# The routing section of a two-layer mixture-of-experts kernel: another way to the gather indices, and another order of loads

## The chip, the cores and the metric

One Trainium2 chip, one of its cores. The metric is the device time of one execution in microseconds, the median of several runs. The profile is that of one execution.

## The reference

There are 1024 tokens of 128 features, in 8 batches of 128. Two layers run one after the other, all in float32; the change lies in the first.

```python
# layer 0: a projection with a weight for each batch, then experts with top 2 of 8
out  = einsum('btc,oc->bto', x, W_base) + b_base
lora = einsum('bter,eor,be->bto', einsum('btc,erc->bter', x, As), Bs, w)
c    = out + 2 * lora
top_w, top_idx = top_k(softmax(c @ router_w.T), 2); top_w /= sum(top_w) + 1e-9
y    = relu(c @ w1[e].T + b1[e]) @ w2[e].T + b2[e]        # hidden width 512
x    = x + sum over the two chosen e of top_w * y
# layer 1: each batch by the expert of its argmax (silu(up) * gate, width 256), then
# every one of 8 experts takes its best 256 tokens (gelu, width 512), scattered back by add
```

## The kernel before

**Routing.** The logits of the router don't need the projected tokens: router and projection are folded into one 128x8 matrix for each batch (`gmat`), and eight matmuls on `xT_sb` give all logits (L468). VectorE picks the top two (L897 to L906). TensorE counts, with triangular and all-ones matrices, how many tokens stand in front of each in its expert (L498 to L503). This gives each (token, choice) a slot in one list of 2048, sorted by expert. VectorE splits the slot's number into block (`blk`, 16 of them) and place in the block (`loc`), and makes two one-hots: `slot1h` (128 places x 16 pairs of choice and batch, L926) and `blk1h` (16 x 16 blocks, L921). `blkv` holds `blk1h` times the token's number in its batch (part 0, on ScalarE, L744) and times the constant `dval`, which is 128 c + 1024 k (part 1, on VectorE, L923). Sixteen matmuls (L512) turn them into the two parts of each slot's number. VectorE adds the parts (L937), turns them to int32 as `sidx` (L938, where a result is scattered to) and masks them to `gidx` (L940, the token to be gathered). `slot1h` compares `loc` with `cols0`, an iota table of 128x2048 in bf16 that ScalarE writes (L736).

**Projection.** It runs beside this. ScalarE scales `b_sb` by the batch's weights (L734). TensorE puts W_base into two banks, by a matmul of `wb_sb` with the identity (L473), and adds the low-rank part (L477, `sum_weights`). ScalarE copies the sum to `w_eff` (L739); TensorE multiplies the tokens by it (L483, `project`); ScalarE copies the result to `c_tok` (L742). The SP queue stores `c_tok` to `rows0` in DRAM, in two halves (L335).

**Experts of layer 0.** Each of the 16 blocks of 128 slots is gathered by GpSimd with an indirect DMA from `rows0` (L394). It waits for `gidx` and for both stores (L383, L384). TensorE turns the block (L523) and runs 23 pairs of block and expert: `up` (L538) and `down0` (L548). In iteration j it turns block j, runs `up` of pair j - 1 and `down0` of pair j - 2; up to 24 full-width matmuls on ones (`keep_warm`, L516) stand before the first. VectorE copies each pair's w1 to a ring (`w1_now`, L951) and keeps the results (L976, L982); GpSimd scatters finished blocks.

**The SP queue**, in order: `first`, `xT`, `consts`, `second`, `crow`, all of w1 (2064 KB), 6 of 8 experts of w2 (1536 KB, L331); then the waits for both halves of `c_tok` and the two stores of 256 KB (L335), the other two experts of w2 (512 KB, L337), `b2`, `gate_w`, `c1`. From L349 on it waits for `cexp` of VectorE and then, paced by the turned blocks, loads the weights of layer 1. TensorE waits for all of w2 before its first `down0` (L562).

**After it**: layer 1 (L566 to L700), which nothing in the diff touches.

Of the kernel before, what the change touches and what calls it, by code (L numbers as in the profile page):

```python
# [27 lines left out]
E = 8  # L28
# [32 lines left out]
           ("slotj", NPAIR), ("dval", K * NC), ("cval", NC), ("same", P), ("coarse", 2), ("steps", STEPS)]  # L61
# [16 lines left out]
def constants():  # L78
# [21 lines left out]
    put("dval", (P * c + T * k).reshape(1, -1))  # L100
# [8 lines left out]
def adaln_moe(nc, xT, x, first, second, rows, w1, w2, cond_w, gate_w, v1, c1, v2, consts, out):  # L109
    with ExitStack() as ctx:  # L110
# [24 lines left out]
        b_sb = sb("b_sb", [P, C])  # L135
# [56 lines left out]
        blkv = sb("blkv", [P, K * NC, 2, NB], BF16)  # L192
        idxf = sb("idxf", [P, NB])
# [77 lines left out]

        dve = sem("dve_steps")
# [47 lines left out]
        def _(sp):  # L320
# [6 lines left out]
            load(b_sb[:], second, in_second)  # L327
            load(crow_sb[:], rows[:, CNR:CNR + NC * E], in_crow)
            load(w1_sb[:], w1, in_w1)
            W2H = 6 * NF * C  # L330
            load(w2_sb[:, 0:W2H], w2[:, 0:W2H], in_w2)  # L331
# [49 lines left out]
        def _(pool):  # L381

# [61 lines left out]
        def _(pe):  # L444
# [26 lines left out]
            pe.wait_ge(in_const, 16)  # L471
            for g in range(2):
                pe.matmul(bank[2 + g][:], wb_sb, ident.unsqueeze(1).to_broadcast([P, 4, P]), start=True, stop=False)  # L473

            def sum_weights(g):
                pe.wait_ge(bsc_ready, 4 * g + 4)
                pe.matmul(bank[2 + g][:], a_sb, bsc[:, 512 * g:512 * g + 512], start=False, stop=True).then_inc(w_summed, 1)  # L477

            def project(g):

                pe.wait_ge(w_eff_ready, g + 1)
                for c in range(4 * g, 4 * g + 4):
                    mm = pe.matmul(bank[5 + g][:, P * (c % 4):P * (c % 4) + P], xT_sb[:, P * c:P * c + P],  # L483
                                   w_eff[:, P * c:P * c + P], start=True, stop=True)
# [10 lines left out]
            sum_weights(1)  # L495
            pe.wait_ge(mask_ready, 1)
# [19 lines left out]
            keep_warm(bank[3], 24)  # L516
# [37 lines left out]
            for j in range(NPAIR + 2):  # L554
# [6 lines left out]
                if j == 2:  # L561
                    pe.wait_ge(in_w2, 32)  # L562
# [166 lines left out]
        def _(act):  # L729
# [3 lines left out]
            for c in range(NC):  # L733
                act.activation(bsc[:, C * c:C * c + C], b_sb[:], ACT.Identity, scale=cr2[:, c:c + 1]).then_inc(bsc_ready, 1)  # L734
            act.wait_ge(in_const, 16)
            act.activation(cols0, const("iota").unsqueeze(2).to_broadcast([P, P, K * NC]), ACT.Copy).then_inc(cols_ready, 1)  # L736
# [15 lines left out]
            act.activation(cols1, const("iota").unsqueeze(2).to_broadcast([P, P, K * NC]), ACT.Copy).then_inc(cols_ready, 1)  # L752
# [107 lines left out]
        def _(v):  # L860
# [61 lines left out]
            v.wait_ge(blk1h_ready, 1)  # L922
# [280 lines left out]
```

## Time and profile before

| | us |
|---|---|
| median of 3 runs | 170.29 |
| lowest and highest of them | 168.7, 170.41 |
| the profiled execution | 169.11 |
| its span in the trace | 167.3 |
| busy in it: TensorE, VectorE, ScalarE, GpSimd | 141.0, 92.5, 72.8, 64.4 |

The span runs from the first instruction to the last; 1.81 us of the execution's own time lie around it. Times of rows are microseconds from the span's start. PE is TensorE, PEld its weight loads, DVE VectorE, ACT ScalarE, POOL GpSimd; SPq is the queue that issues DMAs. "Issue" is time for which the profile shows nothing that was waited for.

### The profile page before, as it was taken

How to read it: one execution, taken by the hardware profiler on the slowest of the kernel's cores; microseconds unless marked ns; L12 is line 12 of the kernel's file. 1: busy time of each engine (PE TensorE's matmuls, PEld its weight loads, DVE VectorE, ACT ScalarE, POOL GpSimd, SP SyncE). 2: the span in 40 equal slices, each digit the busy share in tenths (PEclk: the TensorE clock that was granted, in tenths of full speed). 3: DMA queues.
4: the chain of work that ended last, by engine and by line, in shares of the span. 5: the costliest groups of instructions: out<-in, count | busy, mean ns of one | idle time of the engine just before them, and what ended most of it. 6: DMA issues, size and time to landing. Idle time of an engine off the chain costs nothing.

```text
span 167.3 us, 3393 instructions
## 1 busy us (share of the span) xinstructions
PE 141.0 (84%) x1044; PEld 117.8 (70%) x1044; DVE 92.5 (55%) x302; ACT 72.8 (44%) x223; POOL 64.4 (38%) x67
## 2 busy tenths in 40 slices
PE   7998959999999999994999720188889988899991
PEld 3756439999988999743999610045479877788990
DVE  0489391565553554415767988764353368436182
ACT  1678325777765656301478540000145444434100
POOL 0000376544476445624000000015777777776000
PEclk9999996999999999999699995559999999999999
DMA  5999827998898921127069240000122345515804
GB/s 163 355 427 345 254 67 218 325 297 277 281 299 246 313 108 47 35 64 220 0 264 402 92 133 0 0 2 21 50 50 66 93 135 173 174 52 157 233 17 125
DMA packets 20419, 27.52 MB, mean 164 GB/s; under 512 B 2034, under 2 KB 14706, under 8 KB 20146
## 3 DMA queue, kind: packets, MB, share of 16 engines
q1 hardware_dynamic: 17410, 22.78, 41.2%
q0 software_dynamic: 1920, 4.00, 8.0%
q10 hardware_dynamic: 1072, 0.52, 1.1%
q8 instruction: 9, 0.15, 0.4%
q14 instruction: 8, 0.07, 0.1%
HBM read 20.71 MB, written 6.59 MB: 163 GB/s over the span
## 4 chain that ended last, share of the span: by engine, by line
PE 55%; DMA 14%; DVE 12%; POOL 9%; issue 6%; ACT 1%; DVEq 0%; ACTq 0%; POOLq 0%
PE bank L538 10%; PE bank L548 9%; PE bank L679 6%; PE bank L580 5%; PE bank L689 4%; PE bank L669 4%; DMA xs<-rows,gidx 4%; DVE bsc L1060 4%; DMA xg<-rows,idx 4%; POOL xg L420 3%; DMA rows<-c_tok 2%; POOL plane L427 2%; PE bank L450 2%; DMA got<-picked 2%; PE bank L589 2%
## 5 line engine op out<-in xcount | busy, mean ns | idle before, releaser
L763 ACT ACTIVATE hT<-bank,w_now 128x128 f32<-128x128 f32 x92 | 26.2, 368 | 13.6 <-PE bank L538 13.6
L394 POOL DMA_INDIRECT xs<-rows,gidx x16 | 15.5, 969 | 27.7 <-DMA rows<-c_tok 18.8
L538 PE MATMUL bank<-xg,w_now 128*128 (+1 forms) x184 | 25.5, 283 | 0.0
L548 PE MATMUL bank<-w_sb,hT 128*128 (+1 forms) x184 | 25.1, 281 | 0.3 <-ACT hT L763 0.3
L548 PEld LDWEIGHTS bank<-w_sb,hT 128*128 128x128 f32 x184 | 23.2, 198 | 0.5 <-ACT hT L763 0.5
L538 PEld LDWEIGHTS bank<-xg,w_now 128*128 128x128 f32 x184 | 23.2, 198 | 0.5 <-issue 0.5
L450 PE MATMUL bank<-ones 128*128 128x512 bf16 x81 | 22.0, 418 | 1.1 <-DVE ones L877 1.1
L842 ACT ACTIVATE h1T<-bank,c_sb 128x256 f32<-128x256 f32 x32 | 13.4, 470 | 19.0 <-PE bank L669 19.0
L399 POOL DMA_INDIRECT picked<-y,sidx x16 | 15.4, 962 | 13.3 <-DVE y L982 12.1
L420 POOL DMA_INDIRECT xg<-rows,idx x16 | 16.9, 1058 | 6.3 <-issue 4.0
L669 PE MATMUL bank<-xgT,v_sb 128*128 128x256 f32 x64 | 16.5, 383 | 0.5 <-ACT xgT L833 0.5
L976 DVE TENSOR_TENSOR yt<-bank,b_sb 128x128 f32<-128x128 f32 x23 | 6.7, 291 | 18.0 <-PE bank L548 15.8
L679 PEld LDWEIGHTS bank<-v_sb,h1T 128*128 128x128 f32 x128 | 15.3, 192 | 1.0 <-ACT h1T L842 0.8
L679 PE MATMUL bank<-v_sb,h1T 128*128 128x128 f32 x128 | 15.9, 277 | 0.1
L427 POOL DMA_INDIRECT plane<-x_sb,idx x12 | 13.6, 1136 | 3.7 <-issue 2.7
L450 PEld LDWEIGHTS bank<-ones 128*128 128x128 bf16 x81 | 8.2, 109 | 9.4 <-issue 2.2
L431 POOL TENSOR_TENSOR hlfv<-hlf1h,cst 128x128 bf16<-128x128 bf16 x1 | 0.8, 776 | 34.5 <-DVE hlf1h L1099 34.5
L1123 DVE TENSOR_TENSOR yb<-bank,c2b_sb 128x128 f32<-128x128 f32 x16 | 4.7, 291 | 15.4 <-issue 9.3
L669 PEld LDWEIGHTS bank<-xgT,v_sb 128*128 128x128 f32 x64 | 11.0, 191 | 1.6 <-ACT xgT L833 0.7
L951 DVE COPY w_now<-w_sb 128x516 f32 (+1 forms) x23 | 11.0, 477 | 1.5 <-issue 1.5
L982 DVE SCALAR_TENSOR_TENSOR y<-yt,pairm,y 128x128 f32 (+1 forms) x23 | 8.1, 351 | 5.6 <-DVE yt L976 5.5
L580 PE MATMUL bank<-x1T,cw_sb 128*128 128x128 f32 x64 | 9.6, 298 | 0.0
(183 smaller groups left out, 208.0 us busy)
## 6 DMA issues: line engine op xcount, KB each, us to landing
v_sb<-in_v SPq DMA_DIRECT2D x16, 256.0 KB
cw_sb<-in_cond_w SPq DMA_DIRECT2D x8, 386.5 KB
plane<-y SPq DMA_DIRECT2D x6, 512.0 KB, 4.7
w_sb<-plane SPq DMA_DIRECT2D x6, 512.0 KB, 4.2
w_sb<-in_w SPq DMA_DIRECT2D x1, 2064.0 KB, 9.1
w_sb<-in_w SPq DMA_DIRECT2D x1, 1536.0 KB, 12.3
rows<-row SPq DMA_DIRECT2D x1, 544.0 KB, 3.4
xT_sb<-in_xT SPq DMA_DIRECT2D x1, 512.0 KB, 3.8
```

The source lines that it names most:

```text
L394: pool.indirect_dma_start(out=xs[:, b % RING], out_offset=None, in_=rows0, in_offset=rows_at(gidx, b)).then_inc(gathered[b % RING], 16)
L399: pool.indirect_dma_start(out=picked, out_offset=rows_at(sidx, b), in_=y0[:, b], in_offset=None).then_inc(scattered, 16)
L420: pool.indirect_dma_start(out=xg[:, i], out_offset=None, in_=rows1, in_offset=rows_at(idx1, i)).then_inc(gathered1[e], 16)
L427: pool.indirect_dma_start(out=plane[e], out_offset=rows_at(idx1, i), in_=y1[:, e % Y1_RING, h], in_offset=None).then_inc(added[e], 16)
L450: pe.matmul(out_bank[:], ones[:], ones[:].unsqueeze(1).to_broadcast([P, 4, P]), start=True, stop=True)
L538: mm = pe.matmul(bank[2 + j % 2][:, P * f:P * f + P], w1_now[:, j % WB_RING, P * f:P * f + P], xsT[:, bass.ds((j - e) * P, P)], start=True ...
L548: mm = pe.matmul(bank[6 + j % 2][:, 0:C], hT[:, j % 2, P * f:P * f + P], w2_sb[:, bass.ds(e * (NF * C) + f * C, C)], start=(f == 0), stop= ...
L580: mm = pe.matmul(bank[2 + b % 2][:, P * m:P * m + P], cw_sb[:, b, P * m:P * m + P], x1T[:, b % 2], start=True, stop=True)
L669: mm = pe.matmul(bank[2 + u % 3][:, CAP * f:CAP * f + CAP], v1_sb[:, e, P * fc:P * fc + P], xgT[:, e % 2], start=True, stop=True)
L679: mm = pe.matmul(bank[6 + h][:, 0:C], h1T[:, e % 2, f, P * h:P * h + P], v2_sb[:, e, f], start=(f == 0), stop=(f == NF - 1))
L763: ins = act.activation(hT[:, j % 2, P * f:P * f + P], bank[2 + j % 2][:, P * f:P * f + P], ACT.Relu, bias=w1_now[:, j % WB_RING, F + f:F + ...
L842: act.activation(h1T[:, e % 2, fc], bank[2 + (2 * e + h) % 3][:, CAP * f:CAP * f + CAP], ACT.Gelu, bias=c1_sb[:, e * NF + fc:e * NF + fc + ...
```

## The change

- The base projection is no longer put into the weights. Eight matmuls of `xT_sb` with `wbT_sb` (W_base turned on the host, loaded with `second`, which grows from 64 to 128 KB) go straight into the banks of the result, and `project` adds the low-rank part on top.
- `cols0` is written by GpSimd instead of ScalarE.
- `blkv` has three parts: the token's number in its batch (ScalarE as before), 128 c, and 1024 k. The last two come from one GpSimd instruction of 512 elements per partition.
- `slot1h` is made in two halves, with a count for each; the 16 matmuls have 48 columns instead of 32 and can begin after the first half.
- `gidx` is one sum of parts 0 and 1 from PSUM to int32. It comes before `pairc`, `pairx` and `exi`, and `sidx` (`gidx` plus part 2) after them.
- `keep_warm` behind them has 14 matmuls instead of 24.
- The first load of w2 holds 3 experts (768 KB) instead of 6; the other 5 (1280 KB) are loaded behind the stores. TensorE waits for the first load at j = 2 and for the second at j = 5.

```diff
-            W2H = 6 * NF * C
-            load(w2_sb[:, 0:W2H], w2[:, 0:W2H], in_w2)
+            W2H = 3 * NF * C
+            load(w2_sb[:, 0:W2H], w2[:, 0:W2H], in_w2_first)
...
         def _(pool):
+            pool.wait_ge(in_const, 16)
+            pool.tensor_copy(cols0, const("iota").unsqueeze(2).to_broadcast([P, P, K * NC])).then_inc(cols_ready, 1)
+            pool.wait_ge(blk1h_ready, 1)
+            pool.tensor_tensor(blkv[:, :, 1:3], blk1h[:].unsqueeze(2).to_broadcast([P, K * NC, 2, NB]),
+                               const("dval").rearrange("p (i v) -> p i v", v=2).unsqueeze(3).to_broadcast([P, K * NC, 2, NB]),
+                               ALU.mult).then_inc(blkv_ready[1], 1)
...
-            pe.wait_ge(in_const, 16)
-            for g in range(2):
-                pe.matmul(bank[2 + g][:], wb_sb, ident.unsqueeze(1).to_broadcast([P, 4, P]), start=True, stop=False)
+            pe.wait_ge(in_second, 16)
+            for c in range(NC):
+                pe.matmul(bank[5 + c // 4][:, P * (c % 4):P * (c % 4) + P], xT_sb[:, P * c:P * c + P], wbT_sb,
+                          start=(c % 4 == 0), stop=False)
...
-                pe.matmul(bank[2 + g][:], a_sb, bsc[:, 512 * g:512 * g + 512], start=False, stop=True).then_inc(w_summed, 1)
+                pe.matmul(bank[2 + g][:], a_sb, bsc[:, 512 * g:512 * g + 512], start=True, stop=True).then_inc(w_summed, 1)
...
-                                   w_eff[:, P * c:P * c + P], start=True, stop=True)
+                                   w_eff[:, P * c:P * c + P], start=False, stop=(c % 4 == 3))
...
-            pe.wait_ge(onehots, 1)
             for i in range(K * NC):
-                mm = pe.matmul(bank[1][:, 0:2 * NB], slot1h[:, :, i], blkv[:, i].rearrange("p v b -> p (v b)"),
+                pe.wait_ge(onehots, i // NC + 1)
+                mm = pe.matmul(bank[4][:, 0:3 * NB], slot1h[:, :, i], blkv[:, i].rearrange("p v b -> p (v b)"),
                                start=(i == 0), stop=(i == K * NC - 1))
-            keep_warm(bank[3], 24)
+            keep_warm(bank[3], 14)
...
                 if j == 2:
-                    pe.wait_ge(in_w2, 32)
+                    pe.wait_ge(in_w2_first, 16)
+                if j == 5:
+                    pe.wait_ge(in_w2, 16)
...
-            act.activation(cols0, const("iota").unsqueeze(2).to_broadcast([P, P, K * NC]), ACT.Copy).then_inc(cols_ready, 1)
...
-            v.wait_ge(blk1h_ready, 1)
-            v.tensor_tensor(blkv[:, :, 1], blk1h[:], bc(const("dval"), 2, NB), ALU.mult).then_inc(blkv_ready[1], 1)
             v.wait_ge(cols_ready, 1)
-            v.tensor_tensor(slot1h[:], cols0, bc(loc[:], 1, P), ALU.is_equal).then_inc(onehots, 1)
+            for k in range(K):
+                v.tensor_tensor(slot1h[:, :, NC * k:NC * k + NC], cols0[:, :, NC * k:NC * k + NC],
+                                bc(loc[:, NC * k:NC * k + NC], 1, P), ALU.is_equal).then_inc(onehots, 1)
...
+            v.wait_ge(slots, 1)
+            int_sum(gidx[:], bank[4][:, 0:2 * NB].rearrange("p (v b) -> p b v", v=2)).then_inc(idx_ready, 1)
             link(v.tensor_tensor(pairc[:], bc(passed[:], 1, NPAIR), bc(const("iota")[:, 0:NPAIR], 2, E), ALU.is_lt))
             link(v.tensor_reduce(pairx[:], pairc[:], AX.X, ALU.add))
             v.tensor_copy(exi[:], pairx[0:1]).then_inc(exi_ready, 1)
-            v.wait_ge(slots, 1)
-            link(v.tensor_reduce(idxf[:], bank[1][:, 0:2 * NB].rearrange("p (v b) -> p b v", v=2), AX.X, ALU.add))
-            v.tensor_copy(sidx[:], idxf[:]).then_inc(sidx_ready, 1)
-            v.wait_ge(sidx_ready, 1)
-            v.tensor_scalar(gidx[:], sidx[:], T - 1, None, ALU.bitwise_and).then_inc(idx_ready, 1)
+            v.wait_ge(idx_ready, 1)
+            v.tensor_tensor(sidx[:], gidx[:], bank[4][:, 2 * NB:3 * NB], ALU.add).then_inc(sidx_ready, 1)
```

## Rows read from the trace of the kernel before

**Rows 1.** Chain that ended last, 12 to 26 us: start, us, what
```profile
14.24 4.13 DMA rows<-c_tok
...
18.41 0.81 issue
19.22 1.27 POOL xs L394
...
20.79 2.51 DMA xs<-rows,gidx
...
23.34 0.33 PE bank L523
```

**Rows 2.** DMA issues by line: count, KB each, median us to landing
```profile
w_sb<-in_w SPq DMA_DIRECT2D x1, 1536.0 KB, 12.3
...
rows<-c_tok SPq DMA_DIRECT2D x2, 256.0 KB, 3.6
...
out_x<-c_tok SPq DMA_DIRECT2D x2, 256.0 KB, 2.4
```

**Rows 3.** Windows: us; PE, PEld, DVE, ACT, POOL busy (x); PEclk; DMA share; GB/s
```profile
9.00:12.00 3.00, 3.00 (x20) 1.53 (x19) 2.34 (x13) 2.51 (x3) 0.00 (x0) 1.00 1.03 438
...
18.40:21.30 2.90, 2.65 (x13) 0.98 (x10) 1.47 (x3) 0.00 (x0) 1.78 (x2) 1.00 0.71 262
21.30:22.00 0.70, 0.00 (x0) 0.00 (x0) 0.70 (x1) 0.00 (x0) 0.45 (x1) 1.00 0.26 70
```

**Rows 4.** Timeline, 2 to 17 us: start, us, engine line, out<-in, [idle <-releaser]
```profile
2.99 0.82 SPq L322 DMA_DIRECT2D w_sb<-in_w  x2
...
5.98 0.23 DVE L886 CAST tri<-cst 128x128 bf16<-128x128 f32 x1 [0.57 <-DMA cst<-in_consts]
...
9.14 1.88 PE L477 MATMUL bank<-bsc,first_sb 128*128 128x512 f32 x4
...
10.67 0.23 DVE L906 TENSOR_TENSOR mask<-sel 128x64 bf16<-128x64 f32 x1
...
11.53 2.05 PE L483 MATMUL bank<-w_eff,xT_sb 128*128 128x128 f32 x16
...
14.72 1.14 PE L512 MATMUL bank<-blkv,slot1h 128*128 128x32 bf16 x16 [0.50 <-ACT blkv L744]
...
15.71 5.34 PE L450 MATMUL bank<-ones 128*128 128x512 bf16 x24
...
16.57 0.17 DVE L940 TENSOR_SCALAR gidx<-sidx 128x16 int32<-128x16 int32 x1
```

**Rows 5.** GpSimd's groups by shape: count | busy us, mean ns | idle before
```profile
L412 POOL MEMSET y<- 128x1024 f32 x1 | 1.0, 951 | 3.5 <-DMA got<-picked 3.5
L431 POOL TENSOR_TENSOR hlfv<-hlf1h,cst 128x128 bf16<-128x128 bf16 x1 | 0.8, 776 | 34.5 <-DVE hlf1h L1099 34.5
```

**Rows 6.** VectorE's line 1103: ns min/median/max, first and last start
```profile
L1103 DVE TENSOR_TENSOR slot1h<-xT_sb,loc x8: 681/681/683, 112.2 to 124.7; 128x1024 bf16<-128x1024 bf16 x8
```

**Rows 7.** Timeline, GpSimd from 110 to 119 us
```profile
112.33 0.78 POOL L431 TENSOR_TENSOR hlfv<-hlf1h,cst 128x128 bf16<-128x128 bf16 x1 [34.48 <-DVE hlf1h L1099]
```

**Rows 8.** Timeline, 15 to 29 us: what is made late and who waits
```profile
15.30 0.35 DVE L932 TENSOR_TENSOR pairc<-passed,cst 128x184 f32<-128x184 f32 x1
...
16.07 0.17 DVE L934 CAST exi<-pairx 1x23 int32<-1x23 f32 x1
...
17.57 0.43 DVE L951 COPY w_now<-w_sb 128x516 f32<-128x516 f32 x1 [0.83 <-issue]
...
28.45 0.29 DVE L976 TENSOR_TENSOR yt<-bank,b_sb 128x128 f32<-128x128 f32 x1 [3.44 <-PE bank L548]
```

**Rows 9.** Tile xs, whole kernel: us from issue to landing
```profile
DMA to landing us min/median/max: 2.4/4.2/4.9
```

**Rows 10.** Windows (columns as in rows 3): TensorE's clock before the experts
```profile
21.05:22.28 1.23, 0.00 (x0) 0.00 (x0) 1.23 (x1) 0.00 (x0) 0.93 (x2) 1.00 0.29 73
...
24.75:28.25 3.50, 3.50 (x17) 3.46 (x17) 0.26 (x1) 2.40 (x9) 2.62 (x3) 0.52 0.64 182
```

More of the change, by code:

```diff
@@ L60 @@
 _WIDTHS = [("ident", P), ("tri", P), ("iota", P), ("rev", E), ("pcol", 1), ("lt", NC * E), ("le", E),
-           ("slotj", NPAIR), ("dval", K * NC), ("cval", NC), ("same", P), ("coarse", 2), ("steps", STEPS)]
+           ("slotj", NPAIR), ("dval", 2 * K * NC), ("cval", NC), ("same", P), ("coarse", 2), ("steps", STEPS)]
 _AT, _n = {}, 0
@@ L99, in constants @@
     k, c = np.meshgrid(np.arange(K), np.arange(NC), indexing="ij")
-    put("dval", (P * c + T * k).reshape(1, -1))
+    put("dval", np.stack([P * c, T * k], axis=2).reshape(1, -1))
     put("cval", P * np.arange(NC)[None, :])
@@ L134, in adaln_moe @@
         bb_sb = first_sb[:, BB:BB + 1]
-        b_sb = sb("b_sb", [P, C])
+        second_sb = sb("second_sb", [P, 2 * C])
+        b_sb, wbT_sb = second_sb[:, 0:C], second_sb[:, C:2 * C]
         w1_sb = sb("w1_sb", [P, E * FW])
@@ L191, in adaln_moe @@
         blk1h = sb("blk1h", [P, K * NC, NB], BF16)
-        blkv = sb("blkv", [P, K * NC, 2, NB], BF16)
-        idxf = sb("idxf", [P, NB])
+        blkv = sb("blkv", [P, K * NC, 3, NB], BF16)
         sidx = sb("sidx", [P, NB], I32)
@@ L270, in adaln_moe @@
         in_gw, in_v, in_crow, in_b2, in_c2b = sem("in_gw"), sem("in_v"), sem("in_crow"), sem("in_b2"), sem("in_c2b")
+        cols1_ready = sem("cols1_ready")
+        in_w2_first = sem("in_w2_first")
         dve = sem("dve_steps")
@@ L326, in _ @@
             load(cst[:], consts, in_const)
-            load(b_sb[:], second, in_second)
+            load(second_sb[:], second, in_second)
             load(crow_sb[:], rows[:, CNR:CNR + NC * E], in_crow)
             load(w1_sb[:], w1, in_w1)
-            W2H = 6 * NF * C
-            load(w2_sb[:, 0:W2H], w2[:, 0:W2H], in_w2)
+            W2H = 3 * NF * C
+            load(w2_sb[:, 0:W2H], w2[:, 0:W2H], in_w2_first)
             for g in range(2):
@@ L495, in _ @@
             sum_weights(1)
+            pe.wait_ge(in_const, 16)
             pe.wait_ge(mask_ready, 1)
@@ L733, in _ @@
             for c in range(NC):
-                act.activation(bsc[:, C * c:C * c + C], b_sb[:], ACT.Identity, scale=cr2[:, c:c + 1]).then_inc(bsc_ready, 1)
+                act.activation(bsc[:, C * c:C * c + C], b_sb, ACT.Identity, scale=cr2[:, c:c + 1]).then_inc(bsc_ready, 1)
             act.wait_ge(in_const, 16)
-            act.activation(cols0, const("iota").unsqueeze(2).to_broadcast([P, P, K * NC]), ACT.Copy).then_inc(cols_ready, 1)
             for g in range(2):
@@ L750, in _ @@
             act.activation(scrap[:], bb_sb, ACT.Silu)
-            act.activation(cols1, const("iota").unsqueeze(2).to_broadcast([P, P, K * NC]), ACT.Copy).then_inc(cols_ready, 1)
+            act.activation(cols1, const("iota").unsqueeze(2).to_broadcast([P, P, K * NC]), ACT.Copy).then_inc(cols1_ready, 1)
             def take_x(b):
@@ L1056, in _ @@
             v.tensor_scalar(coarse_enough[:], coarse_sum[:], float(CAP), None, ALU.is_ge).then_inc(enough_ready, 1)
-            v.wait_ge(cols_ready, 2)
+            v.wait_ge(cols1_ready, 1)
             for s in range(STEPS):
@@ L1178 @@
             a(L0_cond_b_base).reshape(C, 1)], axis=1),
-        "second": a(L0_cond_Bs).transpose(0, 2, 1).reshape(E * R, C),
+        "second": np.concatenate([a(L0_cond_Bs).transpose(0, 2, 1).reshape(E * R, C), a(L0_cond_W_base).T], axis=1),
         "w1": np.concatenate([a(L0_ffn_w1).transpose(2, 0, 1), a(L0_ffn_b1).reshape(E, NF, P).transpose(2, 0, 1)],
```

## The prediction

> **What bounds the kernel now.** I read the page's busy table and its 40 slices first: TensorE is at 84% and gapless over most of the kernel, so the time can only move where TensorE waits for something or runs at half clock. The change touches the first 25 us, so I read the chain that ended last there [rows 1]. The reader is to see that it leaves the compute engines at 14.24 us, when the second half of `c_tok` is evicted. It then follows the store of that half to DRAM for 4.13 us, to 18.37 us, 0.81 us of issue, the first gather on GpSimd (1.27 us), the second gather's 2.51 us to landing, and comes back to TensorE at 23.34 us. The indices were complete at 16.57 + 0.17 = 16.74 us [rows 4], and GpSimd waits for both; so the store ends the wait, 18.37 - 16.74 = 1.6 us after the indices.
>
> Next: why does that store take 4.13 us? By the DMA table the same bytes (`out_x`, 256 KB) land in 2.4 us where nothing else moves, and the two stores here in 3.6 us at the median [rows 2], so the first one in about 2 x 3.6 - 4.13 = 3.1 us. The load of six w2 experts is the second of two issues from 2.99 to 3.81 us [rows 4], so it went out at 3.4 us, and lands 12.3 us later, at 15.7 us [rows 2]: the stores stand behind it. Transfers run on to 21.3 us and then all but end [rows 3]. From then on the loop of experts is TensorE's own, so what the loop starts earlier, the kernel ends earlier, up to changes of the clock.
>
> **The change part by part.**
>
> 1. *Base projection.* Removed: L473, 4 passes of 512 columns, the shape of L477, which took 1.88 us. Added: 8 matmuls of 128 columns, 16 passes, the shape of L483, which took 2.05 us [rows 4]. TensorE reaches `sum_weights` 0.1 to 0.2 us later. L477 ended at 9.14 + 1.88 = 11.02 us and the counts, which wait for `mask` at 10.90, follow: the cover was 0.1 us, so I charge +0.15 us on `c_tok` and the counts. It also waits for `second`, now 128 KB, but it stands right behind the constants, which were in at 5.98 us; 64 KB more at 438 GB/s [rows 3, 4] are 0.15 us, and TensorE wants it only behind the logits. Nothing.
>
> 2. *`cols0` to GpSimd.* ScalarE's copy lay between `bsc` and `w_eff`. `w_eff` can come a little earlier now, but `project` stands behind the counts on TensorE and can't. Nothing gained. GpSimd has no row of such a copy. Nearest is a memset of 1024 elements in 0.95 us [rows 5]: 1.9 us for 2048, and I let it be double, 3.8 us. It starts at 6.0 us (constants [rows 4]), ends at 7.9 to 9.8 us, and is wanted at 13.0 us. Cover 3 us.
>
> 3. *`blkv` parts on GpSimd, `slot1h` in halves.* VectorE loses part 1 of `blkv` and makes `slot1h` in two of about 0.65 us: a half has the size of L1103, 0.68 us [rows 6]. First half at 13.7, second at 14.35 us. GpSimd's product of 512 elements has one neighbour, 128 elements in 0.78 us [rows 5]: 0.8 us if all is fixed, 3.1 us if all is per element. I take 1.8 us, between them, because at the memset's rate 128 elements are 0.12 us, so a good part of 0.78 must be per instruction. VectorE has `blk1h` at 13.0 us, and `blkv` is then complete at 13.0 + 1.8 = 14.8 us (bounds 13.8 and 16.1). Part 0 on ScalarE, which released the matmuls at 14.72 us [rows 4], comes 0.15 us later with `c_tok`. The 16 matmuls take 1.1 us as now (their cost is the weights' load), 14.9 to 16.1 us.
> The row says 0.78 us for 128 elements. The Trainium skill (GPSIMD Engine Reference, § Performance versus the Vector engine) puts a two-input operation there at about 2.6 cycles per element at 1.2 GHz: an estimate from that page is 1.1 us for 512 elements plus a fixed part, which agrees better with my 1.8 than with the linear 3.1; the sum doesn't use it.
>
> 4. *Indices.* Three dependent instructions, the last ending at 16.74 us, become one of 0.17 us, and it no longer stands behind `exi` (16.07 us) [rows 4, 8]: `gidx` at 16.1 + 0.05 + 0.17 = 16.4 us instead of 16.74 (bounds 15.4 and 17.7 by GpSimd's). The store was 1.6 us behind the indices, so by itself this gives nothing; it matters once the store lands near 17. Queued behind the waiting sum on VectorE are now `pairc`, `pairx`, `exi`, 15.30 to 16.24 = 0.94 us [rows 8], so `exi` at 17.3 instead of 16.24 us, 1.1 us later. Behind it stand `w_now` (17.57, to 18.6) [rows 8], the clearing of `y0`, and `cexp`, which releases SP's weight loads. TensorE's first `up` wants `w_now` at about 22.4 us; the end of this tail is wanted by the first `yt`, before which VectorE sat idle 3.44 us [rows 8]. 1.1 us late plus a loop 0.9 us early are 2.0 us: covered. SP starts the layer 1 loads 1 us later; they are paced by the loop and catch up.
>
> 5. *w2 behind the stores.* 768 KB leave the front of the queue: 0.79 MB at 438 GB/s are 1.8 us, so the first part of w2 lands at 13.9 us instead of 15.7, before or just as the stores come. The second store is issued at 14.39 us. Its landing lies between 2.4 us (idle engines) and 4.13 us (as now) [rows 1, 2]. I take 2.8 us, between the idle price and the 3.1 us of the first store, since in front of it is only the first store and behind it 1.8 MB are queued. It lands at 17.2 us instead of 18.37: 1.2 us earlier, 0.8 us behind the indices. With 0.81 us of issue, the first gather starts at 18.0 us, the second at 18.0 + 1.27 + 0.3 = 19.6 us.
> The bytes that were in front are now beside the gathers. Before, the second gather started at 20.79 us and had the quiet of 21.3 us on [rows 3]: 2.51 us. Among transfers the median is 4.2 and the least 2.4 us [rows 1, 9]. The total of bytes is the same and ends at about 21.5 us, so the second gather, 19.6 us, is half in traffic: 2.8 us (bounds 2.4 and 4.2), landing at 22.4 instead of 23.34 us. Gain 0.9 us.
> In `down0` the wait at j = 2 is for 768 KB, long landed; the wait at j = 5 comes 8 us later than the last transfer. `b2` follows 0.79 MB later in the same queue than its bytes did, but all ends by about 21.5 us, and `yt` wants it at 27 us.
>
> 6. *`keep_warm` 14 instead of 24.* It ends at 16.1 + 14 x 0.22 = 19.2 us instead of 21.05 [rows 4, 10]. TensorE then has nothing until the first gather at about 21 us. Before, the clock fell to 0.52, the 1.2 GHz level, from 24.75 to 28.25 us, after the loose stretch 21.05 to 24 us, and came back [rows 10]. At half clock the 3.5 us did about half of their work: 1.7 us lost. After the change the loose stretch is 19.2 to 22.5 us, about as long, so I forecast one such fall of the same length: no difference, with bounds from -1.7 us (no fall) to +1.7 us (two).
>
> **Sum** on the profiled execution: 169.11 - 0.9 = 168.2 us. That execution is 1.18 us below the median 170.29; against the median it is 169.4 us. I predict 169.3 us, as the bounds of the clock lean a little down: the fall can hardly be longer than the 3.5 us without a longer gap, while it may move into the waits.
>
> **The rivals.**
>
> - *The clock takes its share with it* (gain 2 to 3 us). The fall comes sooner, while TensorE still waits for its gathers, and costs the loop only part of 1.7 us. 0.9 + 1.2 = 2.1 us or more: 168.2 us or less against the median. For: the falls are 3.5 us long and TensorE's idle now starts 1.8 us earlier and ends 0.9 us earlier. Against: nothing sets where it falls, and a longer gap is no reason for a shorter fall.
> - *GpSimd's tables become the bound* (no change). At 3.1 us for `blkv`, or more beside VectorE's `slot1h`, `gidx` comes at 17.7 us and the first gather starts at 18.5 us, 0.7 us earlier than now; with a second gather of 3.2 us for 2.51 nothing is left: about 170.3 us. For: the one row of such a product is dear. Against: the part of it that is fixed.
> - *The shared port* (slower). GpSimd's copy of `cols0`, 6.0 to 8 or 10 us, lies beside VectorE's chain that ends with `mask` at 10.9 us [rows 4], which now had nothing beside it, and most of its instructions read two SBUF operands. If GpSimd holds VectorE off, the whole chain, `mask`, the counts, `blkv` and `project` come up to 2.2 us later, against 0.9 gained: 171.6 us. It decides once the delay is over 0.9 us, that is, once the copy takes over 2.5 us and excludes VectorE fully. Against it: L1103, two SBUF operands, ran at 112.16 us beside GpSimd's product (112.33 to 113.11 us) [rows 6, 7], and all its eight instances took 681 to 683 ns. VectorE wasn't slowed at all there. The Trainium skill (GPSIMD Engine Reference, § Key points) says that GpSimd "shares its SBUF interfaces with VectorE" and contends with instructions of two SBUF inputs; on VectorE's side this trace doesn't bear it out, so its chance is small.
> - *Traffic takes all of it* (no change or slightly slower). The first two gathers take 4.2 us: the second lands at 23.8 us, 0.5 us later than now: 170.8 us.
>
> **How the numbers follow.** Forecast as summed (168.7 to 170.0 us): 0.42. Clock takes its share: 0.30. GpSimd's tables: 0.10. Traffic: 0.08. Shared port or a second fall of the clock (171 to 172 us): 0.10. About 1% is what a measurement of this kernel tells from no change, here 1.7 us; the three runs shown lie 1.7 us apart. Faster by more: the clock case and a seventh of the forecast, 0.36. Slower by more: 0.12. Within: 0.52. The range from 166.8 us (no fall of the clock, and store and gather at their least, 0.4 us each: 170.29 - 0.9 - 1.7 - 0.8) to 171.0 us leaves out half of the slower cases and a little of the fastest.
>
> **What would show each step.** Right: the chain still goes c_tok, store, gather; the store's piece is 2.4 to 3.1 us and lands near 17.2 us; GpSimd's product takes 1.2 to 2.4 us; `gidx` ends at 16.2 to 16.6 us; the second gather lands near 22.4 us; the instructions before `mask` keep the like of L906's 0.23 us. Wrong: GpSimd released by VectorE's `gidx` instead of the store (tables or port), gathers of 4 us, L473's successor or the copy on GpSimd ending after 13 us, or a clock of 0.5 for 7 us after 20 us.

## The result and the profile after

| | before | after |
|---|---|---|
| median us (range, runs) | 169.5 (168.63 to 170.41, 4) | 172.17 (170.94 to 173.87, 4) |
| profiled execution, us | 169.11 | 172.31 |
| its span, us | 167.3 | 170.4 |
| its mean granted clock | 0.939 | 0.926 |

The ratio is 1.02 with the interval [1.0154, 1.0247]: slower by about 2%, where 169.3 us was forecast, a small gain on the 170.29 us of before. Runs over 1.5% above the fastest of their kernel are left out of every ratio, here and below (two runs are left of a_cols_act, b_warm14 and a_warm24_again, three of a_w2_six and a_warm24_cols_act), so a ratio can differ from the quotient of the medians, which is 1.016 here. The page of the kernel after, its busy table and two of its rows in 40 slices:

```profile
span 170.4 us, 3400 instructions
PE 139.9 (82%) x1046; PEld 118.9 (70%) x1046; DVE 94.0 (55%) x301; ACT 71.1 (42%) x222; POOL 67.3 (39%) x69
...
PEclk9999965999999999999699985559999999999998
```

The dip in the `PEclk` row's first quarter, 65, stands at 21 to 30 us; in the same row of before it is a single 6, at 26 to 30 us. The chain that ended last, from the constants to the first experts (start us, us, what), answers to [rows 1]:

```profile
6.29 0.23 DVE tri L898
6.51 1.45 DVE same L899
7.96 0.30 issue
...
11.59 0.23 DVE mask L918
...
14.59 0.61 ACT c_tok L754
...
15.21 2.84 DMA rows<-c_tok
...
18.90 1.15 POOL xs L403
...
20.36 4.40 DMA xs<-rows,gidx
24.80 0.47 PE bank L534
```

From the eviction of `c_tok` to the first experts both chains have the same links, and four of them changed. The store is issued at 15.21 instead of 14.24 us [rows 1]. It takes 2.84 instead of 4.13 us, so it lands 0.32 us earlier, at 18.05 us. The second gather starts 0.43 us earlier, but takes 4.40 instead of 2.51 us, and TensorE turns its block at 24.80 instead of 23.34 us: 1.46 us later (the first block at 24.08 instead of 22.29, 1.79 us later). Further up, the chain now passes through VectorE's casts, which it didn't before. The timeline of the kernel after, with what each waited for:

```profile
6.32 1.94 POOL L386 CAST y<-cst 128x2048 bf16<-128x2048 f32 x1 [5.87 <-DMA cst<-in_consts]
6.43 1.91 DVE L899 CAST same<-cst 128x128 bf16<-128x128 f32 x1
8.27 0.22 DVE L901 CAST iota<-cst 128x128 bf16<-128x128 f32 x1
8.51 0.21 DVE L907 TENSOR_TENSOR lg<-bank,gmat 128x64 f32<-128x64 f32 x1
11.59 0.22 DVE L918 TENSOR_TENSOR mask<-sel 128x64 bf16<-128x64 f32 x1
11.96 0.16 PE L509 MATMUL bank<-ones,mask 128*64 128x1 bf16 x1 [0.45 <-DVE mask L918]
14.04 1.43 POOL L388 TENSOR_TENSOR blkv<-blk1h,cst 128x512 bf16<-128x512 bf16 x1 [5.78 <-DVE blk1h L933]
15.64 1.19 PE L523 MATMUL bank<-blkv,slot1h 128*128 128x48 bf16 x16 [0.44 <-ACT blkv L756]
16.93 0.19 DVE L887 TENSOR_REDUCE gidx<-bank 128x16 int32<-128x32 f32 x1 [0.23 <-PE bank L523]
```

The cast of `same`, 128x128 from fp32 to bf16, takes 1.91 us, while its twin into `iota` takes 0.22 us. It started 0.11 us after GpSimd's copy and ended 0.08 us after it. Row L509 has the price of this at its end: TensorE, which went straight from the base sum to the counts before, waited 0.45 us for `mask`. The two tables of one-hots repeat the picture on a smaller scale (by tile: count, then min/median/max ns and first and last start):

```profile
L937 DVE TENSOR_TENSOR slot1h<-y,loc x2: 684/1112/1539, 13.9 to 14.5; 128x1024 bf16<-128x1024 bf16 x2
```

The half that started before GpSimd's product (14.04 us) took 0.68 us beside it; the one that started during it took 1.54 us, and ended 0.55 us after the product.

The product was most likely held in its turn. It always starts inside VectorE's first half, and its length depends on how far inside: 1.43 us where it starts 0.17 us into it (six profiles), 1.35 us where it starts 0.24 us into it (the six with `cols0` on ScalarE, here a_cols_act, whose first half started at 14.60 us):

```profile
14.84 1.35 POOL L387 TENSOR_TENSOR blkv<-blk1h,cst 128x512 bf16<-128x512 bf16 x1 [14.39 <-DVE blk1h L933]
```

In all twelve it ends 0.91 us after VectorE's first half, as if it began its own work only then. No profile has a product with nothing of VectorE beside it.

The last view is TensorE's clock (window, its length, PE busy with its instructions, granted clock, DMA share, GB/s):

```profile
20.00:22.00 2.00, 0.00 (x0) 1.00 0.96 383
22.00:24.00 2.00, 0.00 (x0) 0.57 0.77 268
24.00:26.00 2.00, 1.68 (x6) 0.50 0.12 33
26.00:28.00 2.00, 2.00 (x11) 0.50 0.22 51
28.00:30.00 2.00, 2.00 (x16) 0.72 0.93 283
```

Read in half microseconds, TensorE stands at the 1.2 GHz level from about 22.3 to 29.1 us: 6.8 us, where it stood there 3.4 us before [rows 10]. The DMA column has the second reading: the transfers run at 383 GB/s until 22 us and at 268 GB/s to 24 us, just while the first two gathers wait for theirs. In [rows 3] that traffic was over by 21.3 us, when the second gather had hardly begun.

From there the delay is carried, and hardly changes over the first nine blocks, although the clock's fall is twice as long: the first block is 1.79 us late, the ninth block is turned at 39.36 instead of 37.73 us (+1.63). Then the table `hlfv` of layer 1 starts at 114.42 instead of 112.33 us (+2.09), and the last sum ends 3.1 us later.

### The profile page after: what moved, and what is told of

Its sections match the earlier page's. It is cut to its first block, busy times and chain, and to the rows that moved or that the text cites. A ratio compares the mean times of both kernels' runs of the same rounds, so it can differ in the third digit from the quotient of the medians.

```text
span 170.4 us, 3400 instructions
## 1 busy us (share of the span) xinstructions
PE 139.9 (82%) x1046; PEld 118.9 (70%) x1046; DVE 94.0 (55%) x301; ACT 71.1 (42%) x222; POOL 67.3 (39%) x69
## 4 chain that ended last, share of the span: by engine, by line
PE 51%; DMA 18%; DVE 16%; POOL 5%; issue 5%; ACT 1%; SPq 0%; DVEq 0%; ACTq 0%; POOLq 0%
PE bank L549 11%; PE bank L559 9%; PE bank L692 7%; DMA xs<-rows,gidx 5%; PE bank L682 5%; PE bank L593 5%; DMA xg<-rows,idx 5%; PE bank L702 4%; DVE bsc L1071 4%; DMA cst<-in_consts 3%; DMA got<-picked 2%; POOL picked L408 2%; PE bank L602 2%; DMA rows<-c_tok 2%; PE bank L662 2%
## 5 line engine op out<-in xcount | busy, mean ns | idle before, releaser
L549 PE MATMUL bank<-xg,w_now 128*128 (+1 forms) x184 | 26.3, 289 | 0.0
L549 PEld LDWEIGHTS bank<-xg,w_now 128*128 128x128 f32 x184 | 24.0, 204 | 0.4 <-issue 0.3
L559 PEld LDWEIGHTS bank<-w_sb,hT 128*128 128x128 f32 x184 | 22.6, 193 | 0.6 <-ACT hT L775 0.5
L459 PE MATMUL bank<-ones 128*128 128x512 bf16 x71 | 19.6, 419 | 1.1 <-DVE ones L889 1.1
L436 POOL DMA_INDIRECT plane<-x_sb,idx x12 | 13.0, 1080 | 4.0 <-issue 2.4
L459 PEld LDWEIGHTS bank<-ones 128*128 128x128 bf16 x71 | 7.3, 110 | 8.2 <-issue 2.2
```

The source lines that it names most:

```text
L436: pool.indirect_dma_start(out=plane[e], out_offset=rows_at(idx1, i), in_=y1[:, e % Y1_RING, h], in_offset=None).then_inc(added[e], 16)
L459: pe.matmul(out_bank[:], ones[:], ones[:].unsqueeze(1).to_broadcast([P, 4, P]), start=True, stop=True)
L549: mm = pe.matmul(bank[2 + j % 2][:, P * f:P * f + P], w1_now[:, j % WB_RING, P * f:P * f + P], xsT[:, bass.ds((j - e) * P, P)], start=True ...
L559: mm = pe.matmul(bank[6 + j % 2][:, 0:C], hT[:, j % 2, P * f:P * f + P], w2_sb[:, bass.ds(e * (NF * C) + f * C, C)], start=(f == 0), stop= ...
```

## The experiments

The runs were made in five series, each with the kernel before beside it. In series 1, 2, 3 and 5 that kernel itself took 181.5 to 184.5 us instead of 169, so only ratios within a series are compared. Series 2 and 4 are both recorded for chip 3, so the level hardly is the chip's. All kernels of the table compute the whole reference.

| kernel | series | median / before, us | ratio [95%] |
|---|---|---|---|
| b_cols_pool | 1 | 182.06 / 181.54 | 1.0124 [1.006, 1.0189] |
| b_w2_three | 1 | 182.46 / 181.54 | 1.006 [1.0001, 1.0119] |
| a_cols_act | 1 | 184.88 / 181.54 | 1.0175 [1.0088, 1.0262] |
| a_w2_six | 1 | 183.65 / 181.54 | 1.0133 [1.008, 1.0187] |
| a_both_undone | 2 | 181.64 / 183.59 | 1.0018 [0.995, 1.0087] |
| a_warm24 | 2 | 181.77 / 183.59 | 0.998 [0.9924, 1.0036] |
| b_warm14 | 2 | 181.01 / 183.59 | 0.9867 [0.9703, 1.0031] |
| b_w2_late | 2 | 183.46 / 183.59 | 1.0126 [1.006, 1.0192] |
| after_again | 3 | 184.04 / 184.35 | 1.0102 [0.9987, 1.0217] |
| a_warm24_cols_act | 3 | 182.71 / 184.35 | 0.9926 [0.979, 1.0063] |
| a_copy_after_casts | 3 | 184.88 / 184.35 | 1.0097 [1.0009, 1.0184] |
| a_best | 3 | 182.78 / 184.35 | 1.0022 [0.994, 1.0103] |
| b_again | 4 | 168.8 / 168.79 | 1.003 [0.999, 1.007] |
| b_warm14_again | 4 | 170.63 / 168.79 | 1.0155 [1.0097, 1.0214] |
| a_warm24_again | 4 | 172.79 / 168.79 | 1.0148 [1.0036, 1.026] |
| a_three_undone | 4 | 170.6 / 168.79 | 1.0125 [1.0058, 1.0193] |
| b_index | 5 | 182.33 / 184.45 | none |
| b_base | 5 | 181.4 / 184.45 | none |

"a_" is the kernel after with something undone, "b_" the kernel before with one part of the change; after_again and b_again are the two kernels unchanged.

Two things weaken the ratios of series 1 to 3. Several aren't borne out by the medians of all runs, whose quotient is 1.003 for b_cols_pool, 0.999 for b_w2_late, 0.998 for after_again and 0.989 for a_both_undone. And the traces of this level have stops that the others don't: in all fourteen profiles from series 1, 2, 3 and 5 TensorE turns the fifteenth block 5.7 to 6.8 us after the fourteenth, in the six near 169 us 1.9 to 2.4 us after it. In b_w2_late, b_base and b_cols_pool the first block is turned at 21.3, 22.5 and 22.6 us, but the fifth only at 30.4, 30.8 and 31.2 us, where b_again has them at 23.4 and 29.6 us. A lead at the front is lost on the way there, so these series say little of what a front is worth at the end. The kernel before has no profile at this level.

**Series 1: the copy and the split, each undone and each alone.** a_cols_act:

```diff
-            pool.tensor_copy(cols0, const("iota")...).then_inc(cols_ready, 1)
+            act.activation(cols0, const("iota")..., ACT.Copy).then_inc(cols_ready, 1)
```

> The changed kernel with cols0 back on ScalarE. Theory P (GpSimd's copy of cols0 holds VectorE's cast of `same` for 1.9 us and makes everything behind it 0.9 us late): the cast is back at 0.22 us, mask ends near 10.9 instead of 11.8 us, the second store is issued near 14.3 instead of 15.2 us, and the time falls by 0.9 us. Theory T (the 1280 KB of w2 that now run beside the first gathers are what costs): the stores move up, but the first two gathers still take 4 to 5 us to land, the loop starts no earlier than now, and the time falls by under 0.4 us.

a_w2_six:

```diff
-            W2H = 3 * NF * C
+            W2H = 6 * NF * C
```

> The changed kernel with six experts of w2 in front of the stores again and two behind. Theory T: the stores take 3.5 to 4 us again, but the second gather lands in about 2.5 us after its start, so the loop starts no later than in the changed kernel, and the time is the same or up to 0.8 us lower. Theory S (the split is worth what it was made for, the store 1.2 us earlier): the time rises by 0.5 to 1.2 us. Theory P says nothing of it.

b_cols_pool is the first diff the other way round, in the kernel before, and b_w2_three likewise the second, with the waits at j = 2 and j = 5 of the change.

> The kernel before with only cols0 moved to GpSimd. Theory P: the cast of `same` takes 1.9 us, mask is 0.9 us later, and as the store is on the chain the time rises by 0.9 us. If the port has no part in it, the time stays within 0.3 us.

> The kernel before with only the load of w2 split at three experts instead of six. Theory T: the store lands 1.2 us earlier (2.8 instead of 4.1 us), the first two gathers land in over 4 us each, the loop starts within 0.5 us of before, the gap in front of it is longer and the time is the same or up to 1 us higher. Theory S: the loop starts 0.9 us earlier and the time falls by 0.9 us.

Alone in the kernel before, GpSimd's copy costs 1.24% by the ratio, though 0.3% by the medians, and the split 0.6%, only just told from nothing. Two rows of b_cols_pool's timeline:

```profile
6.11 1.94 POOL L384 CAST y<-cst 128x2048 bf16<-128x2048 f32 x1 [5.66 <-DMA cst<-in_consts]
6.22 1.91 DVE L889 CAST same<-cst 128x128 bf16<-128x128 f32 x1
```

The held cast is there with GpSimd's copy alone. In all six profiles whose copy starts as soon as the constants are in, `same` takes 1.91 us; with the copy on ScalarE, or behind the casts, it takes 0.22 us. What it costs at the end of the chain is TensorE's wait for `mask`: 0.45 us in the kernel after, 0.28 in after_again, 0.37 in b_cols_pool, 0.93 in a_warm24 and 1.32 in a_warm24_again, the more the later the constants land against the logits (VectorE's first cast starts 0.30, 0.13, 0.23, 0.78 and 1.17 us behind the first logits there). In a_w2_six TensorE itself came later than `mask`.

Undoing one of the two isn't told from the kernel after: 1.0175 and 1.0133 beside 1.02. Both profiles have a fall of the clock that the other two of this series don't have, here a_cols_act's, in the columns of the clock's view above:

```profile
7.00:9.00 2.00, 2.00 (x13) 0.63 0.92 363
9.00:11.00 2.00, 2.00 (x11) 0.52 0.97 408
```

The base projection (L481, 16 passes) took 3.61 us in it where it takes 2.03, and the store was issued at 15.94 us though `mask` had started at 10.68, as before. TensorE was busy without a gap there, and a_both_undone, the same kernel but for one number, has a clock of 1.00 in the same windows. I found no cause; a fall of about 3.4 us in this place hit three of the twenty profiles (b_index is the third). These three began their logits at 5.56 or 5.57 us, earlier than any other but the first profile of the kernel before, which began at 5.57 us and has no such fall. It hides what the two were to show, in these profiles at least.

**Series 2: both undone, the warm-ups, and the rest of w2 later still.** a_both_undone takes both edits; a_warm24 and b_warm14 change one number; b_w2_late moves a load:

```diff
-            keep_warm(bank[3], 14)
+            keep_warm(bank[3], 24)
...
-            load(w2_sb[:, W2H:], w2[:, W2H:], in_w2)
             load(b2_sb[:], ...)
             load(c1_sb[:], c1, in_gw)
+            sp.wait_ge(x_turned, 2)
+            load(w2_sb[:, W2H:], w2[:, W2H:], in_w2)
```

> The changed kernel with cols0 on ScalarE and six experts of w2 in front. If port and traffic are the causes and add, this is within 0.5% of the kernel before, although the indices, the halves, the base projection and the 14 warm-ups are still the changed ones. Theory C (the shorter row of warm-ups, through a longer fall of the clock) expects it still 0.5% to 1% slower than before.

> The changed kernel with 24 warm-ups instead of 14. Theory C: TensorE's idle in front of the loop shrinks by 2.2 us, the clock at 1.2 GHz covers no more than the 3.5 us of before instead of 6.3 us, and the time falls by about 1 us (ratio to before 1.012 to 1.015 instead of 1.02). If the gap is set by the late gathers alone, ratio 1.02 as it was.

> The kernel before with 14 warm-ups instead of 24. Theory C: 1.8 us more idle in front of the loop, and 0.5 to 1 us slower. Without it: within 0.3 us, as the warm-ups do no work.

> The kernel before with w2 split at three experts, but the other five loaded only once two blocks have been gathered and turned; b2, the gate's weights and c1 stay behind the stores. Theory T: the store lands 1.2 us earlier as in the split alone, and now the second gather lands within 3 us of its start instead of 4.5: the loop starts about 1.2 us earlier and the time falls by 0.6 to 1.4 us. If the gathers are slow for another reason than the traffic of w2, no better than the split alone (ratio 1.006).

With both undone the time isn't told from the kernel before (1.0018). That doesn't prove that nothing is left of the change (see the medians above). The chain of b_w2_late shows the gather's price gone, beside that of b_w2_three:

```profile
14.65 2.63 DMA rows<-c_tok
...
18.13 1.26 POOL xs L396
...
19.70 2.96 DMA xs<-rows,gidx
```

```profile
14.94 2.66 DMA rows<-c_tok
...
18.45 1.25 POOL xs L395
...
20.00 4.50 DMA xs<-rows,gidx
```

The same store, nearly the same start of the gather; 2.96 us where the late w2 isn't queued beside it (25 to 74 GB/s from 19 to 23 us), 4.50 us where it is (328 to 385 GB/s). The end doesn't follow, at 1.0126: its first block is turned 2.7 us before b_w2_three's, its ninth 0.8 us (38.02 against 38.77). A wait of 2.00 us called issue at 27.44 us stands on its chain, the stop before the fifth block named above; b_cols_pool, where no load was moved, has it too.

**Series 3: repeats and combinations.** In a_copy_after_casts GpSimd waits for VectorE's last cast before its copy; a_warm24_cols_act has two edits from above, and a_best adds the later load to them.

```diff
             pool.wait_ge(in_const, 16)
+            pool.wait_ge(casts_done, 1)
             pool.tensor_copy(cols0, const("iota")...).then_inc(cols_ready, 1)
```

> The changed kernel once more, beside the others on one chip. Both theories: ratio to before 1.015 to 1.025 as measured first; the cast of `same` at 1.9 us, the clock at 1.2 GHz for about 7 us around the first blocks.

> The changed kernel with 24 warm-ups and cols0 on ScalarE; the split of w2 stays. Theory C and P together: 2 us or more below the changed kernel, ratio to before about 1.00 to 1.006, as the split alone was. If the split were worth 1 us by itself: 0.995 or less.

> The changed kernel, but GpSimd starts its copy of cols0 only when VectorE's four casts of constants are done. Theory P in its narrow form (only VectorE's casts and copies within SBUF are held, its two-operand float32 instructions are not): no cast over 0.3 us, every step from `lg` to `mask` keeps 0.22 us beside the copy, mask ends 0.9 us earlier, ratio 1.012 to 1.016. In its wide form (two-operand instructions are held too): one or more steps between `lg` and `mask` grow to over 1 us and nothing is gained.

> The changed kernel with cols0 on ScalarE, 24 warm-ups, and the five late experts of w2 loaded only when two blocks are turned. If traffic, port and clock are all that was wrong: store lands near 17 us, second gather near 22 us, no fall of the clock longer than 3.5 us, ratio to before 0.990 to 0.995. If w2 so late starves the loop or the weight loads behind it: 1.00 or more, with TensorE waiting for a DMA at the pair of j = 5 or later.

a_copy_after_casts is the cleanest look at what GpSimd holds:

```profile
6.05 0.22 DVE L901 CAST same<-cst 128x128 bf16<-128x128 f32 x1
6.66 1.89 POOL L388 CAST y<-cst 128x2048 bf16<-128x2048 f32 x1 [6.22 <-DVE ltle L904]
7.80 0.23 DVE L909 TENSOR_TENSOR lg<-bank,gmat 128x64 f32<-128x64 f32 x1 [1.27 <-PE bank L479]
8.06 0.22 DVE L913 TENSOR_REDUCE top<-lg 128x8 f32<-128x64 f32 x1
8.31 0.32 DVE L914 TENSOR_TENSOR eq<-lg,top 128x64 f32<-128x64 f32 x1
8.66 0.22 DVE L915 TENSOR_TENSOR eq<-eq,cst 128x64 f32<-128x64 f32 x1
```

The copy runs from 6.66 to 8.55 us. `lg`, with one operand in PSUM, and the reduction run through it at 0.23 and 0.22 us. The first `eq`, two operands in SBUF, starts at 8.31 and ends at 8.63 us, 0.08 us after the copy. Its 0.32 us are 0.1 us more than the 0.23 us of the second `eq` of this line, at 9.95 us, so a step with two SBUF operands may have been held for the little that was left of the copy. TensorE's wait for `mask` is gone. Its time stays at 1.0097; the gather (4.69 us) and 14 warm-ups with their 6.8 us of half clock are still in it. The kernel after itself, repeated as after_again, is at 1.0102 [0.9987, 1.0217] in this series: below the 1.015 to 1.025 that I expected, and not told from the kernel before, though its trace has the cast of 1.91 us, a first gather of 5.31 us and 6.8 us of half clock. So the edits of this series can't be told from it either. a_warm24_cols_act and a_best are not told from the kernel before, nor clearly from the kernel after. No version beat the kernel before.

**Series 4: the noise, and the warm-ups again.** b_again is the kernel before, unchanged; a_three_undone has the copy on ScalarE, six experts in front and 24 warm-ups, so that the base projection and the index part are left of the change.

> The kernel before once more, for its trace beside the others of one chip. Both theories: ratio 1.00, the cast of `same` at 0.22 us, second gather landed in under 4 us, a fall of the clock of at most 3.5 us in front of the loop.

> The kernel before with 14 warm-ups, repeated since its first interval was 3% wide. Theory C: the clock at 1.2 GHz for about 7 us as in the first trace, ratio 1.005 to 1.012. If the warm-ups are worth nothing: 0.995 to 1.003.

> The changed kernel with 24 warm-ups, repeated. Theory C: a fall of the clock of 3.5 us or none, ratio 0.998 to 1.006. If the first measurement (0.998) was chance: 1.012 or more.

> The changed kernel with 24 warm-ups, cols0 on ScalarE and six experts of w2 in front. If these three are all the causes: ratio 0.995 to 1.003, second gather landed in under 4 us, cast 0.22 us, store behind as in the kernel before. If the base projection, the halves or the new order of the indices cost something of their own: 1.006 or more.

b_again gives 1.003 [0.999, 1.007]: here differences of 1% stand out. 14 warm-ups alone cost 1.55% (1.1% by the medians). The granted clocks of the runs go with it: 0.932 on average over its six, 0.945 over the 17 of the kernel before. That is 1.3% of 168 us, 2.2 us, of clock. In a_warm24_again the clock is back (0.944), and it is slower by 1.48% all the same. The clock of b_again and of b_warm14_again:

```profile
22.00:24.00 2.00, 0.48 (x2) 1.00 0.20 60
24.00:26.00 2.00, 1.71 (x14) 1.00 0.22 66
26.00:28.00 2.00, 1.84 (x17) 1.00 0.45 110
```

```profile
22.00:24.00 2.00, 1.05 (x4) 0.88 0.22 68
24.00:26.00 2.00, 2.00 (x12) 0.50 0.19 57
26.00:28.00 2.00, 2.00 (x15) 0.76 0.47 92
```

The kernel before has no fall at all here, where its first profile had one of 3.4 us; and b_warm14_again has 3.4 us where I expected 7. Over all profiles: with 14 warm-ups (8 kernels) the clock is at its lower level for 6.8 us in six and for 3.4 us in two; with 24 (12 kernels) for 3.4 us in the front of the loop in four, about as long but only at 30 us in one, and not at all in the others.

a_three_undone is the miss of this study. I expected the time of the kernel before, and it is slower by 1.25%, though without a fall of the clock in this place. It is ahead of b_again when the loop finds its pace (a block turned at 27.00 instead of 27.71 us), and loses that at the sixteenth gather (turned at 51.94 instead of 51.17 us). Its chain, then b_again's:

```profile
46.14 5.75 DMA xs<-rows,gidx
51.89 0.04 issue
51.94 0.33 PE bank L533
```

```profile
44.26 4.63 DMA xs<-rows,gidx
48.89 0.04 issue
48.94 0.33 PE bank L523
```

Its last gather is slow and ends the wait alone. SP's loads for layer 1 run beside it; whether their new place against the loop is the cause, wasn't tried. Nor is this where its end comes from: the table `hlfv` of layer 1 starts at 111.67 us, 0.11 us before b_again's, and the 0.9 us by which its span is longer (167.9 against 167.1) arise behind it.

**Series 5: the two parts that were left, each alone.**

> The kernel before with only the part that makes the indices taken from the changed one: three parts of blkv, two of them on GpSimd, slot1h in halves, gidx before exi, sidx last. cols0, w2, the base projection and the 24 warm-ups are those of before. Theory F (a fourth cause lies here: exi, w_now and cexp come about 1 us later): ratio 1.006 or more. If the indices cost nothing, since the store comes after them: 0.997 to 1.004, with the second half of slot1h at 1.5 us beside GpSimd's product.

> The kernel before with only the base projection done as in the changed one. My price was +0.15 us: ratio 0.998 to 1.004. If the fourth cause is here, for instance by a wait for the larger `second`: 1.006 or more, and L477 starting over 0.3 us later than in the kernel before.

The kernel before itself ran from 177.67 to 187.28 us in this series, so there is no interval and nothing is decided. The second half of `slot1h` took 1.54 us in b_index, as expected. A part of what makes that level is seen on the chain of b_base in layer 1:

```profile
133.28 0.44 PE bank L651 x8
133.72 3.26 issue
136.98 0.41 PE bank L660 x2
```

TensorE waits 3.26 us for nothing that the profile shows. On the chains of the six profiles near 169 us none is over 1.2 us.

## Why the prediction was wrong, step by step

Right: the base projection costs what was said (2.03 us for 16 passes, next to none on the path). GpSimd's copy took 1.94 us (forecast 1.9 to 3.8) and its product 1.43 us (1.8, within its bounds, but by luck: some 0.5 us of it is probably GpSimd's own wait for VectorE, and so is most of the 0.78 us in [rows 5] that I took for a fixed cost). The first half of the one-hots took 0.68 us (0.65), the 16 matmuls 1.19 us (1.1), the store 2.84 us (2.8). The store still ends the wait behind the indices, by 0.9 us (0.8), although these ended at 17.12 us where 16.4 was forecast.

**The term of +0.97 us at the store that wasn't in the sum.** The store is issued 0.97 us later where 0.15 was forecast. Three things make it. TensorE's first logits start at 5.99 instead of 5.57 us: 0.42 us, and not the change's, since that start lies anywhere from 5.56 to 6.72 us in the profiles of both kinds of kernel (6.48 in b_again). The base projection makes 0.1 us. The wait for `mask` makes the other 0.45 us, and this is the change's.

**Part 2, "Nothing gained ... Cover 3 us", is the step that failed there.** I checked the copy against the time at which `cols0` is wanted, and not against what VectorE does while it runs. The rival "the shared port" had the mechanism, and I gave it little for two reasons, both wrong. I expected the held instructions to be the two-operand steps before `mask`; they start when the copy has ended, and what was caught was a cast ahead of them in VectorE's queue, which I never priced. And L1103 beside GpSimd's product [rows 6, 7] was no evidence of peace: it started at 112.16 us, before the product at 112.33, and the one that waited was probably the product, which ends 0.26 us after it in every profile. An instruction that is already running isn't held, one that starts during GpSimd's is held to its end, as the two halves of `slot1h` show in one row each way. The price was 2.2 us in the rival and 0.3 to 1.3 us in the traces.

The Trainium skill says this plainly (SBUF — State Buffer, § SBUF: two separate sides): whichever instruction starts first has the shared pair of ports for its whole length and the other is blocked. It adds (§ Who interferes with whom) that copies and casts can come under it too. The trace agrees, with 0.22 against 1.91 us and 0.68 against 1.54 us.

**Part 5: the gain of the store was sized from one profile, and the gather's price too low.** The store with six experts in front takes 4.13 us in the first profile and 4.33 in one more, but 2.78 to 3.08 us in the seven others whose chain shows it (2.80 in b_again, the same kernel). With three in front it takes 2.63 to 2.97 us in nine, and 3.90 in a_best. Most of the 1.3 us that I took as won wasn't there to win. The second gather was to take 2.8 us, "half in traffic", and took 4.40. Its 2.51 us before were one profile's as well: in b_again, the same kernel, the chain runs through the first gather, with 4.63 us. The sum of both is best read from the store's issue to the first turned block, over the profiles whose chains show both ends: 7.4 to 8.5 us in nine with six experts in front (mean 7.9), 8.9 to 9.3 us in eight with three (mean 9.1), and 6.7 and 7.6 us in the two where the rest of w2 is later still. (b_index, with six in front, has another chain; its timeline gives 8.8 us.) The ranges don't touch: the split costs 1.1 us there, where a gain was forecast. That is the rival "traffic takes all of it", priced too low at 4.2 us and at a chance of 0.08. This is the largest step that failed: part 5 put a gain of 0.9 us where there is a loss of that size. That the bytes beside the gathers are the cause is shown by b_w2_late, one profile, and borne out by a_best, whose second gather starts at 21.39 us and whose block is turned at 23.95; for the end of the kernel the split is worth 0.6%, with an interval that reaches almost to nothing.

**Part 6: "one such fall of the same length".** It was twice the length, 6.8 us. The reason that I gave in the sum, that it "can hardly be longer ... without a longer gap", fell on its premise: the gap did grow. The later store and the gathers put the first real work at 24.08 us instead of 22.29, and the warm-ups end at 19.85 instead of 21.05 us, so TensorE is idle for 4.2 us instead of 1.2. But its price isn't in the result. By the prediction's bound another 3.4 us at half clock is 1.7 us, and 1.8 us of this fall pass before TensorE has anything to do. From the first turned block to the ninth the kernel after needs 15.28 us and the kernel before, with its 3.4 us, 15.44; b_again and a_three_undone, without a fall, need 13.77 us, b_warm14_again and a_warm24_again, with 3.4 us, 14.85 and 14.69. So a fall costs 0.9 to 1.7 us there, and the longer one no more than the one it replaced: that the sum put nothing here came out by luck. That ten warm-ups fewer cost something in the kernel before is shown by b_warm14_again (1.0155, with the lower clock of its runs), though its profile is only 0.7 us longer than b_again's. The first measurement, 0.9867 [0.9703, 1.0031], rests on two runs and doesn't bear it out. In the kernel after, a_warm24 (0.998) and a_warm24_again (1.0148) disagree, so what the warm-ups give back there is open.

**What the parts add up to, and what stays open.** The first turned block is 1.79 us late: 0.97 us at the store's issue (0.42 us of it chance, 0.1 the base projection, 0.45 the copy) and 0.82 us from there to the block (8.87 instead of 8.05 us), which fits the split's price. A gain of 0.9 us was forecast. The ninth block is 1.63 us late, `hlfv` 2.09 us, the end 3.1 us. So the front explains more than half of the 3.1 us in these two executions. About 0.5 us more appear between the ninth block and `hlfv`, and 1.0 us only in layer 1's experts, where the gathers of `xg` on the chain take 3.51 and 4.29 us instead of 2.91 and 3.43; no run shows why. Nor do the experiments close the sum: undone singly the parts gave nothing that is told, with all three undone 1.25% is left in one series (a_three_undone), with two undone nothing is in another (a_both_undone). One premise of the first part is also weaker than it was put: an earlier loop isn't always an earlier end, as b_w2_late shows between its fourth and fifth block. So the hold and the price of the split are shown in the traces, and of the single parts only the warm-ups have, at the end of the kernel, an interval above 1 that the medians of the same series bear out, and an earlier measurement doesn't agree. How the parts combine, and what the base and index parts cost, is open.

## What to carry to other kernels

Before work moves to GpSimd, list what VectorE starts while it runs, casts and copies ahead in its queue included, and look for rows where VectorE's instruction starts second: one that started first tells nothing. Bytes taken from in front of a store come out beside whatever follows it, so price the next small transfer and not only the store. Warm-ups are to be counted against the first real matmul of the kernel as changed, and a longer fall of the clock costs only where the engine has work. A term of a sum that rests on a single transfer's time wants a second profile of the same kernel first.

## What the runs showed of the hardware

- In these traces GpSimd held VectorE only for instructions that started during its own: a cast of 128 elements went from 0.22 to 1.91 us, a product of 1024 from 0.68 to 1.54 us. An instruction with an operand in PSUM and a reduction weren't held (0.23 and 0.22 us).
- GpSimd's product of 512 elements took 1.35 or 1.43 us by how far into VectorE's instruction it started, and ended 0.91 us after that one in twelve of twelve profiles.
- The gather of 64 KB that the chain waits for took 2.4 to 3.0 us where little else moved, 3.5 to 4.6 us in six profiles with 0.5 MB of w2 behind the stores, and 4.4 to 5.3 us beside 1.3 MB.
- The clock's falls at the front came in two lengths, 3.4 and 6.8 us, and in three profiles there was one at 7.5 to 11 us, while TensorE was busy without a gap.
- One kernel took 169 us in some series and 181 to 184 us in others, with series of both levels recorded for chip 3. All fourteen profiles of that level have one turned block 5.7 to 6.8 us behind the one before it (1.9 to 2.4 us in the six others), and some have waits of 1 to 5 us on the chain that no row explains.
